# The last tile of a decoder layer: gated rows copied and multiplied in pieces, fewer identity turnings, and a tie factor joined to a multiplication

## The chip, the cores and the metric

The kernel is written in Bass for one NeuronCore of a Trainium2 chip and runs on that one core. What counts is the device time of one execution in microseconds. The kernel before took 554.35 us (median of three runs, 554.33 to 556.05). The engines by their short names: PE is TensorE, DVE VectorE, ACT ScalarE, POOL GpSimd, SP SyncE, which here only issues loads and stores.

## The reference

One layer of a decoder on x of 1024 rows by 128: self-attention with 16 heads, cross-attention of the 1024 rows to 6404 rows of context under a mask, and a feed-forward part whose operands are quantised to four bits in blocks of 16. The change touches only the last.

```python
def fp4_quant_dequant(x):
    xb = x.reshape(shape[:-1] + (shape[-1] // BLOCK, BLOCK))
    scale = jnp.max(jnp.abs(xb), axis=-1, keepdims=True) / 6.0
    scale = jnp.maximum(scale, jnp.float32(1e-12))
    xn = xb / scale
    idx = jnp.searchsorted(_MID, jnp.abs(xn))
    q = _GRID[idx] * jnp.sign(xn) * scale
...
x = x + _L0_xattn_ref(_layernorm(x, axis=-1), ctx_1024, mask_BxSxS2_ik0, L0_xattn_W, L0_xattn_b)
x = x + _L0_ffn_ref(_layernorm(x, axis=-1), ...)
# in _L0_ffn_ref, with fp4_linear(x, w) = quantised x times quantised w:
gate = fp4_linear(x, w_gate)
y = fp4_linear(x, w_up)
h = jax.nn.silu(gate) * y
return fp4_linear(h, w_down)
```

The grid is 0, 0.5, 1, 1.5, 2, 3, 4, 6, and a value in the middle between two points goes to the lower one.

## The kernel before

The five engines each run a program that is written out by hand, in the order in which its instructions stand; semaphores alone tie them together. The rows are cut into 8 tiles of 128. The self-attention takes the first half of the time; the change does not touch it.

**Cross-attention of a tile t.** The context is cut into 13 chunks of 512 columns. For each chunk PE makes the logits in one of two banks (`logits`, three products), DVE adds the mask, takes the maximum and writes them to SBUF (`masked`, L878), ACT takes the exponential, PE turns them (L1240), ACT copies them (L690) and PE multiplies them with the context (`pv_chunk`). The logits run ahead of the rest by seven chunks and a tile. A bank of logits is free for PE when L878 on it is done. POOL makes summands out of the mask's integers in pieces of 1024 columns (L524); SP loads the pieces into a ring of four. At the end of a tile DVE adds the result to x (`finish_tile`, L893).

**Feed-forward of a tile**, `ffn_step(t, c)`, is woven into the chunks c of the next tile's cross-attention on every engine. Step 0: mean and variance on DVE, the root on POOL (L511). Step 1: DVE normalises (L923) and quantises xn. Step 3: PE turns xn (L1280), ACT copies it (L710). Step 4: the gate product and ACT's tanh (L713). Steps 5 and 6: DVE makes the gated rows out of gate and up (L928, L933). Steps 7 and 8: DVE quantises them, 352 columns. Step 9: PE turns them in three pieces (128, 128 and 96 columns, L1293) into bank 7, and ACT copies the three pieces to hT (L718). Step 10: PE multiplies the three pieces with the down weights into bank 7. Step 11: DVE adds the product to x (L942), and SP stores it. PE does these products with the helper at L975, which so carries most matmuls; one 128x128 product in float32 shows as two matmuls.

`quantize` (L898) is a chain of instructions of DVE, each waiting for the one before (`link`): the greatest of each block of 16 (L905), the scale (L906), its reciprocal (L907), times the factor `TIE_DOWN`, a little below one, so that ties go down (L908), the rows times that (L909); then four steps that round to the grid (L911 to L914) and the multiplication with the scale (L915). It runs twice for each tile, on 8 blocks of xn and on 22 blocks of gated rows, and at step 1 it stands in DVE's order ahead of the `masked` of the same chunk.

**The last tile** has no cross-attention beside its feed-forward part. There PE fills two waits with turnings of the identity into a bank nobody reads (`keep_warm`, L978): `TAIL_NORM` of them ahead of all, and `TAIL_HIDDEN` ahead of step 9. Its up product goes to bank 6, right behind the gate.

```python
pv_chunk(NT * NC - 1)
keep_warm(TAIL_NORM, 0)
for c in range(NC):
    if c == 9:
        keep_warm(TAIL_HIDDEN, 0)
    ffn_step(NT - 1, c)
```

Of the kernel before, what the change touches and what calls it, by code (L numbers as in the profile page):

```python
# [7 lines left out]
ALU = mybir.AluOpType  # L8
# [25 lines left out]
def decoder_layer(nc, x, ctx, mask, w_q, w_k, w_v, w_o, w_down_kv, w_up_k, w_up_v,  # L34
# [6 lines left out]
    NT = S // P  # L41
# [30 lines left out]
    EARLY_MASKS = 6  # L72
    WARM_UP = 28
    KEEP_WARM = 4
    TAIL_NORM = 44
    TAIL_HIDDEN = 56
    LEAD = 7

    with ExitStack() as stack:
# [219 lines left out]

        def logits_bank(n):  # L300
            return 4 + n % 2 if n < NC else n % 2

        def up_bank(t):
            return 6 if t == NT - 1 else 7
# [262 lines left out]
        def _(act):  # L567
# [139 lines left out]
            def ffn_step(t, c):  # L707
                if c == 3:
                    act.wait_ge(s_f4, t + 1)
                    act.activation(xqT[:, :], PS[:, 7, 0:P], ACT.Copy).then_inc(s_f5, 1)  # L710
                if c == 4:
                    act.wait_ge(s_f6, 2 * t + 1)
                    act.activation(fa[:, 0, :], PS[:, 7, 0:FF], ACT.Tanh, scale=0.5).then_inc(s_f7, 1)  # L713
                if c == 9:
                    act.wait_ge(s_f9, t + 1)
                    for j in range(NF):
                        w = min(P, FF - j * P)
                        last = act.activation(hT[0:w, j, :], PS[0:w, 7, j * P:(j + 1) * P], ACT.Copy)  # L718
                    last.then_inc(s_f10, 1)

            for e in range(NE):
# [19 lines left out]
        def _(dve):  # L741
            chain = [0]

            def link(ins):
                chain[0] += 1
                ins.then_inc(dch, 1)
                dve.wait_ge(dch, chain[0])
# [150 lines left out]
            def quantize(dst, src, rows, nb, done, parts=(0, 1)):  # L898
                xs = src.rearrange("p (b k) -> p b k", k=BLOCK)
                sc, inv = f_small[0:rows, 0, 0:nb], f_small[0:rows, 1, 0:nb]  # L900
                wide = lambda a: a.unsqueeze(2).broadcast_to([rows, nb, BLOCK])
                v, pw, s2 = (fa[0:rows, i, 0:nb * BLOCK] for i in (1, 2, 3))
                b3 = lambda a: a.rearrange("p (b k) -> p b k", k=BLOCK)
                if 0 in parts:
                    link(dve.tensor_reduce(sc, xs, axis=AX.X, op=ALU.max, apply_absolute_value=True))  # L905
                    link(dve.tensor_scalar(sc, sc, 1.0 / 6.0, 1e-12, ALU.mult, ALU.max))  # L906
                    link(dve.reciprocal(inv, sc))  # L907
                    link(dve.tensor_scalar(inv, inv, TIE_DOWN, None, ALU.mult))  # L908
                    link(dve.tensor_tensor(b3(v), xs, wide(inv), ALU.mult))  # L909
                if 1 in parts:  # L910
                    link(dve.tensor_scalar(pw.bitcast(I32), v.bitcast(I32), 0x7F800000, None, ALU.bitwise_and))  # L911
                    link(dve.tensor_scalar(pw, pw, 1.0, ROUNDER, ALU.max, ALU.mult))
                    link(dve.tensor_tensor(s2, v, pw, ALU.add))  # L913
                    link(dve.tensor_tensor(v, s2, pw, ALU.subtract))  # L914
                    dve.tensor_tensor(b3(dst), b3(v), wide(sc), ALU.mult).then_inc(done, 1)  # L915

            def ffn_step(t, c):
                if c == 0:
                    moments(t, x_sb[:, t, :])
                    dve.tensor_scalar(mv[:, t, 1:2], mv[:, t, 1:2], LN_EPS, None, ALU.add).then_inc(s_f1, 1)  # L920
                if c == 1:
                    dve.wait_ge(s_f2, t + 1)
                    link(dve.tensor_scalar(xn[:, t, :], x_sb[:, t, :], mv[:, t, 0:1], rstd[:, t:t + 1],  # L923
                                           ALU.subtract, ALU.mult))
                    quantize(xn[:, t, :], xn[:, t, :], P, D // BLOCK, s_f3)
                if c == 5:
                    dve.wait_ge(s_f7, t + 1)
                    dve.scalar_tensor_tensor(fb[:, 0, :], fa[:, 0, :], 1.0, PS[:, 7, 0:FF], ALU.add,  # L928
                                             ALU.mult).then_inc(s_fg, 1)
                if c == 6:  # L930
                    dve.wait_ge(s_f6, 2 * t + 2)
                    dve.wait_ge(s_fg, t + 1)
                    dve.scalar_tensor_tensor(fb[:, 1, :], fb[:, 0, :], 0.5, PS[:, up_bank(t), 0:FF], ALU.mult,  # L933
                                             ALU.mult).then_inc(s_fh, 1)
                if c == 7:
                    dve.wait_ge(s_fh, t + 1)
                    quantize(fb[:, 2, :], fb[:, 1, :], P, FF // BLOCK, s_f8, (0,))
                if c == 8:
                    quantize(fb[:, 2, :], fb[:, 1, :], P, FF // BLOCK, s_f8, (1,))
                if c == 11:  # L940
                    dve.wait_ge(s_f11, t + 1)
                    dve.tensor_tensor(x_sb[:, t, :], x_sb[:, t, :], PS[:, 7, 0:D], ALU.add).then_inc(s_f12, 1)  # L942

            for s in range(EARLY_SLOTS):
                if early_rows(s) is not None:
# [27 lines left out]
        def _(pe):  # L973
            def mm(o, a, b, start=True, stop=True, alone=False):
                return pe.matmul(o, a, b, start=start, stop=stop, skip_group_check=alone)  # L975
# [297 lines left out]
            def ffn_step(t, c):  # L1273
                if c == 3:
                    pe.wait_ge(s_f3, t + 1)
                    if t == 0:
                        pe.wait_ge(s_fwc, 2 * NF + 1)
                    else:
                        pe.wait_ge(s_f12, t)
                    pe.transpose(PS[:, 7, 0:P], xn[:, t, :], ident[:, :]).then_inc(s_f4, 1)  # L1280
                if c == 4:
                    pe.wait_ge(s_f5, t + 1)
                    mm(PS[:, 7, 0:FF], xqT[:, :], wguT[:, 0, :]).then_inc(s_f6, 1)
                    if t == NT - 1:
                        mm(PS[:, up_bank(t), 0:FF], xqT[:, :], wguT[:, 1, :]).then_inc(s_f6, 1)
                if c == 6 and t < NT - 1:
                    pe.wait_ge(s_fg, t + 1)
                    mm(PS[:, up_bank(t), 0:FF], xqT[:, :], wguT[:, 1, :]).then_inc(s_f6, 1)
                if c == 9:
                    pe.wait_ge(s_f8, t + 1)  # L1290
                    for j in range(NF):
                        w = min(P, FF - j * P)
                        last = pe.transpose(PS[0:w, 7, j * P:(j + 1) * P], fb[:, 2, j * P:j * P + w], ident[:, :])  # L1293
                    last.then_inc(s_f9, 1)
                if c == 10:
                    pe.wait_ge(s_f10, t + 1)
                    for j in range(NF):
                        w = min(P, FF - j * P)
                        last = mm(PS[:, 7, 0:D], hT[0:w, j, :], wdT[0:w, j, :], start=(j == 0), stop=(j == NF - 1))
                    last.then_inc(s_f11, 1)  # L1300

            for t in range(4, NT):
# [47 lines left out]
```

## Time and profile before

| what | value |
|---|---|
| runs | 554.35, 556.05, 554.33 us |
| the profiled execution | 554.33 us |
| its span, first to last instruction | 552.6 us |
| mean granted clock of PE | 0.963 of full speed |
| PE, DVE, ACT, POOL busy | 499.6 (90%), 362.4 (66%), 336.2 (61%), 171.1 (31%) us |
| chain that ended last, by engine | PE 72%, DVE 20%, issue 3%, DMA 2%, ACT 2% |

The span is 1.7 us shorter than the execution's own time. A granted clock of 1.00 is PE's level of 2.4 GHz, 0.50 that of 1.2 GHz; a mean between the two says that a part of the stretch ran at the lower one. A busy share is a mean over stages with different limits, so it does not tell what a change in one place is worth.

### The profile page before, as it was taken

How to read it: one execution, taken by the hardware profiler on the slowest of the kernel's cores; microseconds unless marked ns; L12 is line 12 of the kernel's file. 1: busy time of each engine (PE TensorE's matmuls, PEld its weight loads, DVE VectorE, ACT ScalarE, POOL GpSimd, SP SyncE). 2: the span in 40 equal slices, each digit the busy share in tenths (PEclk: the TensorE clock that was granted, in tenths of full speed). 3: DMA queues.
4: the chain of work that ended last, by engine and by line, in shares of the span. 5: the costliest groups of instructions: out<-in, count | busy, mean ns of one | idle time of the engine just before them, and what ended most of it. 6: DMA issues, size and time to landing. Idle time of an engine off the chain costs nothing.

```text
span 552.6 us, 9809 instructions
## 1 busy us (share of the span) xinstructions
PE 499.6 (90%) x3494; PEld 327.1 (59%) x3494; DVE 362.4 (66%) x874; ACT 336.2 (61%) x659; POOL 171.1 (31%) x292
## 2 busy tenths in 40 slices
PE   8359999999999999989979979989797997989997
PEld 7206333333333333324549979879797997878886
DVE  6889988888788878704454466646666465654344
ACT  4627778787778777876664826537373562737420
POOL 6810125444444453235442221321222122210000
PEclk9758999999999999999999989989999998999999
DMA  8985400051007000031696423333342333300000
GB/s 243 284 256 121 88 2 2 4 134 41 1 3 166 10 2 2 1 117 39 165 325 187 124 76 116 93 114 92 83 121 79 116 91 115 114 16 6 1 6 7
DMA packets 27957, 49.23 MB, mean 89 GB/s; under 512 B 4140, under 2 KB 15860, under 8 KB 27332
## 3 DMA queue, kind: packets, MB, share of 16 engines
q1 hardware_dynamic: 27156, 47.87, 31.3%
q0 software_dynamic: 224, 0.54, 0.4%
q8 instruction: 28, 0.46, 0.4%
q10 hardware_dynamic: 528, 0.18, 0.2%
q14 instruction: 21, 0.17, 0.1%
HBM read 43.67 MB, written 4.72 MB: 88 GB/s over the span
## 4 chain that ended last, share of the span: by engine, by line
PE 72%; DVE 20%; issue 3%; DMA 2%; ACT 2%; POOL 1%; SPq 0%; DVEq 0%; ACTq 0%; POOLq 0%
PE banks L975 48%; PE banks L1084 11%; PE banks L1240 6%; DVE banks L802 6%; PE banks L1095 2%; DVE logits L878 2%; DVE fa L914 1%; PE banks L980 1%; DMA operands<-query_parts 1%; DVE qc_lo L849 1%; DVE xn L923 1%; DVE fa L913 1%; DVE fa L909 1%; ACT probs L669 1%; DVE f_small L905 1%
## 5 line engine op out<-in xcount | busy, mean ns | idle before, releaser
L669 ACT ACTIVATE probs<-banks 128x512 f32<-128x512 f32 x288 | 160.2, 599 | 49.1 <-PE banks L975 43.5
L802 DVE CUSTOM_DVE_ANT_0 banks<-banks,decay 128x1024 f32<-128x1024 f32 x128 | 155.0, 1244 | 31.4 <-PE banks L975 30.8
L975 PE MATMUL banks<-operands 112*128 112x512 bf16 (+4 forms) x736 | 148.0, 332 | 21.2 <-DMA operands<-query_parts 14.2
L975 PEld LDWEIGHTS banks<-operands 115*128 115x128 bf16 (+1 forms) x736 | 55.2, 98 | 126.9 <-ACT probs L669 55.1
L975 PEld LDWEIGHTS banks<-mem,pT 128*128 128x128 f32 (+1 forms) x816 | 108.5, 196 | 7.9
L975 PE MATMUL banks<-mem,pT 128*128 128x128 f32 (+1 forms) x816 | 112.1, 280 | 0.0
L690 ACT ACTIVATE pT<-banks 128x512 f32<-128x512 f32 (+1 forms) x104 | 60.4, 581 | 53.7 <-PE banks L1240 53.7
L878 DVE CUSTOM_DVE_ANT_0 logits<-banks,mring 128x512 f32<-128x512 f32 (+1 forms) x85 | 56.2, 667 | 43.2 <-PE banks L975 22.0
L532 POOL TENSOR_SCALAR_AFFINE_SELECT probs<-probs 128x128 f32<-128x128 f32 x128 | 37.3, 294 | 108.8 <-ACT probs L669 106.9
L1084 PE MATMUL banks<-probs,v_ext 128*32 128x512 f32 x512 | 68.2, 605 | 0.1
L975 PE MATMUL banks<-memT_hi,qc_hi 128*128 128x512 f32 (+1 forms) x104 | 51.0, 491 | 18.7 <-DVE cmax L878 18.7
L524 POOL TENSOR_SCALAR mring<-mring 128x1024 f32<-128x1024 int32 (+1 forms) x46 | 43.8, 953 | 75.0 <-DMA mring<-in_mask_BxSxS_ik 72.9
L1240 PE MATMUL banks<-ident,logits 128*128 128x128 f32 (+1 forms) x408 | 63.2, 278 | 0.0
L680 ACT ACTIVATE logits<-logits,neg_max 128x1024 f32<-128x1024 f32 (+1 forms) x56 | 58.8, 1050 | 0.0
L1240 PEld LDWEIGHTS banks<-ident,logits 128*128 128x128 f32 (+1 forms) x408 | 49.4, 144 | 4.1 <-issue 2.2
L511 POOL TENSOR_TENSOR rstd<-mv,half_neg 128x1 f32<-128x1 f32 x16 | 8.8, 551 | 129.7 <-DVE mv L920 83.6
L975 PE MATMUL banks<-memT_hi,qc_lo 128*128 128x512 f32 (+1 forms) x104 | 41.3, 397 | 0.0
L975 PE MATMUL banks<-memT_lo,qc_hi 128*128 128x512 f32 (+1 forms) x104 | 41.2, 396 | 0.0
L538 POOL TENSOR_SCALAR_AFFINE_SELECT probs<-probs 128x512 f32<-128x512 f32 x32 | 20.5, 641 | 42.7 <-ACT probs L669 42.7
L975 PEld LDWEIGHTS banks<-memT_hi,qc_hi 128*128 128x128 f32 x104 | 20.5, 198 | 21.5 <-DVE cmax L878 20.9
L710 ACT ACTIVATE xqT<-banks 128x128 f32<-128x128 f32 x8 | 2.2, 278 | 36.8 <-PE banks L1280 36.8
L975 PEld LDWEIGHTS banks<-memT_hi,qc_lo 128*128 128x128 f32 x104 | 20.2, 194 | 4.4
(170 smaller groups left out, 515.4 us busy)
## 6 DMA issues: line engine op xcount, KB each, us to landing
mring<-in_mask_BxSxS_ik SPq DMA_DIRECT2D x39, 512.0 KB, 3.5
operands<-key_parts SPq DMA_DIRECT2D x24, 192.0 KB
operands<-query_parts SPq DMA_DIRECT2D x21, 192.0 KB
key_parts<-operand_parts SPq DMA_DIRECT2D x10, 256.0 KB, 3.3
mem<-in_ctx SPq DMA_DIRECT2D x3, 832.0 KB, 8.9
mask<-in_mask_BxSxS_ik SPq DMA_DIRECT2D x9, 256.0 KB, 2.9
pT<-in_mask_BxSxS_ik SPq DMA_DIRECT2D x9, 256.0 KB, 3.0
query_parts<-operand_parts SPq DMA_DIRECT2D x4, 384.0 KB, 5.3
```

The costliest lines, as they stand in the source:

```text
L524: pool.tensor_scalar(src.bitcast(F32), src, -1.0, -NEG, ALU.add, ALU.mult).then_inc(s_ma, 1)
L532: pool.affine_select(out=diag, in_=diag, compare_op=ALU.is_ge, fill=0.0, base=0, pattern=[[1, P]], channel_multiplier=-1).then_inc(s_sel, 1)
L538: pool.affine_select(out=upper, in_=upper, compare_op=ALU.is_ge, fill=0.0, base=-1, pattern=[[0, HG], [-1, P]], channel_multiplier=1).then ...
L669: act.activation(probs[:, to, :], PS[:, u % 3, :], ACT.Exp).then_inc(s_p, 1)
L680: act.activation(y, y, ACT.Exp, bias=neg_max[:, t:t + 1], accum_out=esum[:, t, e:e + 1]).then_inc(s_e, 1)
L690: last = act.activation(pT[:, n % 3, 0:o], PS[:, 2 + n % 2, 0:o], ACT.Copy)
L802: dve.tensor_tensor_reduce(out=rows, in0=rows, in1=decay[:, off:off + S], scale=1.0, scalar=-3.0e38, op0=ALU.mult, op1=ALU.max, accum_out= ...
L878: dve.tensor_tensor_reduce(out=logits_sb(t)[:, k0:k0 + kw], in0=PS[:, logits_bank(n), 0:kw], in1=mk, scale=1.0, scalar=-3.0e38, op0=ALU.ad ...
L975: return pe.matmul(o, a, b, start=start, stop=stop, skip_group_check=alone)
L1084: last = pe.matmul(PS[h * VW:(h + 1) * VW, 3, :], v_ext[:, kt, g * HG + h, :], probs[:, (gb % 2) * HG + i, :], start=(b % NT == 0), stop=( ...
L1095: last = pe.matmul(PS[h * VW:(h + 1) * VW, 3, d0:d0 + P], v_ext[:, kt, g * HG + h, :], probs[:, 2 * HG + n % 2, h * P:(h + 1) * P], start= ...
L1240: last = pe.transpose(PS[0:kw, 2 + n % 2, j * P:(j + 1) * P], logits_sb(t)[:, k * P:k * P + kw], ident[:, :])
```

## The change

Three edits, and numbers that go with them:

- `quantize` joins the factor to the multiplication: L908 and L909 become one scalar_tensor_tensor, (xs times `TIE_DOWN`) times the reciprocal. This holds for all 16 quantisations of DVE.
- In the last tile ACT signals each of its three copies, PE waits for each piece ahead of the piece's product, and the product goes to bank 6 (`down_bank`), from where DVE adds it.
- `TAIL_NORM` goes from 44 to 40, `TAIL_HIDDEN` from 56 to 46.

```diff
-    TAIL_NORM = 44
-    TAIL_HIDDEN = 56
+    TAIL_NORM = 40
+    TAIL_HIDDEN = 46
...
+        def down_bank(t):
+            return 6 if t == NT - 1 else 7
...
                     for j in range(NF):
                         w = min(P, FF - j * P)
                         last = act.activation(hT[0:w, j, :], PS[0:w, 7, j * P:(j + 1) * P], ACT.Copy)
+                        if t == NT - 1 and j < NF - 1:
+                            last.then_inc(s_f10, 1)
                     last.then_inc(s_f10, 1)
...
-                    link(dve.tensor_scalar(inv, inv, TIE_DOWN, None, ALU.mult))
-                    link(dve.tensor_tensor(b3(v), xs, wide(inv), ALU.mult))
+                    link(dve.scalar_tensor_tensor(b3(v), xs, TIE_DOWN, wide(inv), ALU.mult, ALU.mult))
...
-                    dve.tensor_tensor(x_sb[:, t, :], x_sb[:, t, :], PS[:, 7, 0:D], ALU.add).then_inc(s_f12, 1)
+                    dve.tensor_tensor(x_sb[:, t, :], x_sb[:, t, :], PS[:, down_bank(t), 0:D], ALU.add).then_inc(s_f12, 1)
...
                 if c == 10:
-                    pe.wait_ge(s_f10, t + 1)
                     for j in range(NF):
+                        if t == NT - 1:
+                            pe.wait_ge(s_f10, t + 1 + j)
+                        elif j == 0:
+                            pe.wait_ge(s_f10, t + 1)
                         w = min(P, FF - j * P)
-                        last = mm(PS[:, 7, 0:D], hT[0:w, j, :], wdT[0:w, j, :], start=(j == 0), stop=(j == NF - 1))
+                        last = mm(PS[:, down_bank(t), 0:D], hT[0:w, j, :], wdT[0:w, j, :], start=(j == 0), stop=(j == NF - 1))
```

In the changed kernel the lines of these functions stand 3 to 5 further down. PE's program at its end, before (L980 turns the identity, L1280 xn, L1293 the gated rows `fb`; hqT_ready is `s_f10`):

```order
L980 MATMUL banks<-ident 128x128 x44
L1280 MATMUL banks<-ident,xn 128x128 [waits y_ready,xq_ready]
L975 MATMUL banks<-wguT,xqT 128x352 [waits xqT_ready]
L975 MATMUL banks<-wguT,xqT 128x352
L980 MATMUL banks<-ident 128x128 x56
L1293 MATMUL banks<-ident,fb 128x128 [waits hq_ready]
L1293 MATMUL banks<-ident,fb 128x128
L1293 MATMUL banks<-ident,fb 96x128
L975 MATMUL banks<-wdT,hT 128x128 [waits hqT_ready]
L975 MATMUL banks<-wdT,hT 128x128 x2
```

The same place of the changed kernel:

```order
L984 MATMUL banks<-ident 128x128 x40
L1284 MATMUL banks<-ident,xn 128x128 [waits y_ready,xq_ready]
L979 MATMUL banks<-wguT,xqT 128x352 [waits xqT_ready]
L979 MATMUL banks<-wguT,xqT 128x352
L984 MATMUL banks<-ident 128x128 x46
L1297 MATMUL banks<-ident,fb 128x128 [waits hq_ready]
L1297 MATMUL banks<-ident,fb 128x128
L1297 MATMUL banks<-ident,fb 96x128
L979 MATMUL banks<-wdT,hT 128x128 [waits hqT_ready] x3
```

Nothing changes its place; the two blocks are shorter, and each of the three down products has a wait of its own. On DVE the chain of a quantisation has 9 instructions where it had 10.

## Rows read from the trace of the kernel before

**Rows 1.** The page, chain that ended last, by line.
```profile
PE banks L975 48%; PE banks L1084 11%; PE banks L1240 6%; DVE banks L802 6%; PE banks L1095 2%; DVE logits L878 2%; DVE fa L914 1%; PE banks L980 1%; DMA operands<-query_parts 1%; DVE qc_lo L849 1%; DVE xn L923 1%; DVE fa L913 1%; DVE fa L909 1%; ACT probs L669 1%; DVE f_small L905 1%
```
**Rows 2.** Busy time by stretch, one stretch a tile (stretch, length, engines, clock).
```profile
353.58:387.32 33.74, 30.93 (x213) 28.16 (x213) 20.62 (x63) 17.26 (x37) 7.80 (x9) 0.95 0.35 101
387.32:419.53 32.21, 29.33 (x213) 26.71 (x213) 20.68 (x63) 17.27 (x37) 7.81 (x9) 1.00 0.36 105
...
513.55:535.06 21.51, 19.59 (x165) 18.43 (x165) 9.30 (x30) 8.31 (x18) 0.55 (x1) 1.00 0.01 4
```
**Rows 3.** Waits of PE, 320 to 552.6 us (us in total, times, longest).
```profile
PE banks L975 <- DVE cmax L878: 16.3, 6, 2.9
PE banks L1293 <- DVE fb L915: 2.5, 3, 0.9
PE banks L1280 <- DVE xn L915: 1.2, 2, 1.0
```
**Rows 4.** Timeline, boundary of tile 1 (start us, length us, engine, line, instruction).
```profile
355.72 1.15 DVE L923 TENSOR_SCALAR xn<-x_sb,mv,rstd 128x128 f32<-128x128 f32 x1
355.75 1.54 POOL L524 TENSOR_SCALAR mring<-mring 128x1024 f32<-128x1024 int32 x2
...
357.67 0.17 DVE L908 TENSOR_SCALAR f_small<-f_small 128x8 f32<-128x8 f32 x1
...
358.73 0.29 DVE L913 TENSOR_TENSOR fa<-fa 128x128 f32<-128x128 f32 x1
359.01 1.04 POOL L524 TENSOR_SCALAR mring<-mring 128x1024 f32<-128x1024 int32 x1 [1.73 <-DMA mring<-in_mask_BxSxS_ik]
359.05 1.14 DVE L914 TENSOR_TENSOR fa<-fa 128x128 f32<-128x128 f32 x1
360.23 0.29 DVE L915 TENSOR_TENSOR xn<-fa,f_small 128x128 f32<-128x128 f32 x1
...
361.18 0.50 PE L975 MATMUL banks<-memT_hi,qc_hi 128*128 128x512 f32 x1 [2.81 <-DVE cmax L878]
```
**Rows 5.** Timeline, boundary of tile 2.
```profile
392.67 0.29 DVE L913 TENSOR_TENSOR fa<-fa 128x128 f32<-128x128 f32 x1
392.81 1.06 POOL L524 TENSOR_SCALAR mring<-mring 128x1024 f32<-128x1024 int32 x1 [2.06 <-DMA mring<-in_mask_BxSxS_ik]
393.00 1.01 DVE L914 TENSOR_TENSOR fa<-fa 128x128 f32<-128x128 f32 x1
```
**Rows 6.** Timeline, boundary of tile 5, DVE.
```profile
492.66 0.29 DVE L914 TENSOR_TENSOR fa<-fa 128x128 f32<-128x128 f32 x1
```
**Rows 7.** Timeline, the last tile's feed-forward part.
```profile
540.07 0.33 PE L1280 MATMUL banks<-ident,xn 128*128 128x128 f32 x1 [0.17 <-DVE xn L915]
...
542.05 6.28 PE L980 MATMUL banks<-ident 128*128 128x128 f32 x56
...
544.43 0.18 DVE L908 TENSOR_SCALAR f_small<-f_small 128x22 f32<-128x22 f32 x1
...
547.08 0.52 DVE L915 TENSOR_TENSOR fb<-fa,f_small 128x352 f32<-128x352 f32 x1
548.06 0.35 PEld L1293 LDWEIGHTS banks<-ident,fb 128*128 128x128 f32 x3
...
548.69 0.60 ACT L718 ACTIVATE hT<-banks 128x128 f32<-128x128 f32 x3 [6.57 <-PE banks L1293]
...
549.35 0.94 PE L975 MATMUL banks<-wdT,hT 128*128 128x128 f32 x6 [0.69 <-ACT hT L718]
```
**Rows 8.** Timeline of ACT, a window that holds only the third copy.
```profile
549.03 0.27 ACT L718 ACTIVATE hT<-banks 96x128 f32<-96x128 f32 x1
```
**Rows 9.** Groups of DVE by line and form (busy us, mean ns, idle before).
```profile
L909 DVE TENSOR_TENSOR fa<-fb,f_small 128x352 f32<-128x352 f32 x8 | 4.2, 525 | 0.3
...
L933 DVE SCALAR_TENSOR_TENSOR fb<-fb,banks 128x352 f32<-128x352 f32 x8 | 4.2, 521 | 17.4 <-PE banks L975 17.3
L893 DVE SCALAR_TENSOR_TENSOR x_sb<-banks,rden,x_sb 128x128 f32<-128x128 f32 x8 | 2.8, 351 | 18.2 <-PE banks L975 18.2
```

## Prediction

> **What bounds the kernel now.** I read first the chain that ended last, by line. The matmuls of the helper line L975 carry most of it, but a fifth of the span is VectorE, spread over lines of about 1% each, the quantisation (L909, L913, L914) among them [rows 1]. The change touches only the feed-forward part, which runs one tile behind the cross-attention, so the question is where that part's VectorE work reaches the path.
>
> The second view is the busy time by stretch, one stretch for each tile, from one addition L893 to the next. TensorE is busy for about 31 us of 33.7; the next tile takes 32.2 us. The difference between these two is not work: both have 213 matmuls, and the granted clock is 0.95 in the one and 1.00 in the other [rows 2]. So a stretch at the lower level of the clock (1.2 instead of 2.4 GHz) costs some 1.6 us of a tile. Of the five such tiles (boundaries 0 to 4) four are like the first row, and only the one from 387.32 is at 1.00.
>
> The third view is what TensorE waited for from 320 us on: six times for the masked logits of L878, 16.3 us in all and 2.9 at the longest, three times for the quantised hidden rows (2.5 us), twice for the quantised input rows (1.2 us) [rows 3]. Nothing else there is large.
>
> The fourth is the timeline at such a wait for L878. The logits' banks are freed by L878, which stands in VectorE's order behind the whole quantisation of xn. TensorE starts at 361.18, right behind the first L878 after L915. Look at L923 and L914: 1.15 and 1.14 us, where the like L913 takes 0.29. Each overlaps a mask piece of POOL (L524, at 355.75 and 359.01); L914 ends 0.14 us after that piece's end [rows 4]. At the next tile's boundary the same holds, with L914 at 393.00 and the piece at 392.81 [rows 5]. I read the boundaries of tiles 0 to 4, and they are alike but for one distance: 0.17 to 0.21 us from the piece's start to L914's at tiles 0, 2, 3 and 4, but only 0.04 at tile 1. At tile 5 no mask is left and L914 takes 0.29 [rows 6].
>
> **The factor joined to the multiplication.** Each of 16 quantisations loses one small instruction. L908 lasts 0.17 us on 8 columns and 0.18 on 22 [rows 4, 7], and behind each link the next instruction starts some 0.03 later (L913 ends at 359.02, L914 starts at 359.05 [rows 4]): 0.20 and 0.21 us. What takes L909's place is a scalar_tensor_tensor. Its price here with two operands from SBUF is not in the trace. Nearest rows: on 128x352 L909 takes 525 ns, and L933, of the new kind with one operand from PSUM, 521; on 128x128 L893, which also takes a scalar per row, 351 [rows 9] against 0.29 of the tensor_tensor L913 [rows 4]. I take no difference, as L933 is nearest in form (an immediate factor); the ends are a gain of nothing and a loss of 0.06 each.
>
> Where does this land? In seven quantisations VectorE is what TensorE waits for, with no piece of POOL between: the hidden rows of tile 4, both quantisations of tiles 5, 6 and 7. Three narrow ones and four wide ones: 3 x 0.20 + 4 x 0.21 = **1.44 us**.
>
> At the boundary of tile 1, L914 would start at 358.85, 0.16 before POOL's piece. L913 at 392.67 started 0.14 before the piece and took its plain 0.29 [rows 5], so L914 gets through, and L915 behind it meets the piece and ends, as L914 did before, 0.14 after it: 360.19 instead of 360.52. That gives **0.33 us** (lower end 0).
>
> At the boundaries of tiles 0, 2, 3 and 4, L914 would start within 0.04 us of the piece's start. L923 at 355.72 started 0.03 before a piece and was held all the same [rows 4]. So L914 is still held, its end is set by POOL, and the saved 0.20 us vanishes: **0** (other end 0.33 each). The piece itself does not move: its load is issued behind the first L878 of the boundary, ahead of the quantisation. Here a rule speaks otherwise. The Trainium skill (SBUF — State Buffer, Who interferes with whom) says of this pair of engines that a VectorE instruction with two SBUF inputs and a GpSimd instruction that reads SBUF exclude each other, the first to issue having the port for its whole length. That the later one waits, the trace agrees; that the first start by the record decides, the row at 355.72 denies. By that rule L914 would pass at tile 0, and at the others on a hundredth of a microsecond, and the sum would be up to 1.3 us larger.
>
> The other quantisations of hidden rows (tiles 0 to 3) end with slack before TensorE's turning, which waits only three times [rows 3]; what hides them is TensorE's own logits and products. Were that cover gone they would give 0.21 us each.
>
> **Fewer identity turnings.** The second block (56) runs from 542.05 to 548.33, so about 0.11 us a turning. VectorE has the hidden rows at 547.60 (L915), yet TensorE's first weight load of them is at 548.06 [rows 7]: the block overruns. Behind a plain wait TensorE starts 0.06 after what it waited for (the products at 549.35, behind copies that end at 549.29), so the overrun costs 548.06 - 547.66 = **0.40 us**. With 46 the block ends 1.1 us sooner, and 0.2 more as all begins sooner: about 547.0, before the rows, now due at 547.60 - 0.41 = 547.19. The first block (44 to 40) did not hold: L1280 waited 0.17 us for xn [rows 7]; the cut of 0.45 keeps that so when xn comes 0.20 sooner. Zero by itself.
>
> **Piece by piece.** Now TensorE waits for the three copies as a whole: 548.69 to 549.29, and starts at 549.35; its six half-products take 0.94 [rows 7]. One copy lasts 0.27 [rows 8], so they start 0.165 apart, and the first is there at +0.27. With the same 0.06 the products start at +0.33 instead of +0.66. The second and third pieces (+0.44, +0.60, and 0.06) are there before their pairs are due (0.11 a half: +0.55, +0.77). Gain **0.33 us**; lower end 0.2 if each of the two added waits costs a hand-over. Writing to bank 6 costs nothing: its last reader is L933, long before; in bank 7 the product would overwrite pieces yet to be copied. Two added semaphore increments on ScalarE hold up nobody. Behind the waits stands only the product itself, and for it only L942 and the last store.
>
> **The sum.** 1.44 + 0.33 + 0.40 + 0.33 = 2.50 us, of which 0.41 + 0.40 + 0.33 = 1.14 falls in the last tile. The profiled execution took 554.33 us (span 552.6), which is also the lowest of the three and 0.02 below their median: **551.8 us**, 0.45% less. About 0.3% (1.7 us) is what a measurement of this kernel can tell from no change. The third run, 556.05, stands 1.7 higher, close to the 1.6 us of one low stretch of the clock.
>
> **The rivals.**
> 1. *The clock decides otherwise.* Waits of 2.8 to 2.9 us ended at the low level at four of the five boundaries of tiles 0 to 4, and not at tile 2, though the waits are of one length [rows 2, 3]. Length alone does not decide, so moving the work by some tenths may win or lose one stretch: 551.8 - 1.7 = 550.1, or 551.8 + 1.7 = 553.5. For it: the spread of the three runs. Against: four waits keep their length to a few hundredths, and the first moves not at all. Chance 0.12 for one fewer, 0.14 for one more.
> 2. *L914 slips ahead of the mask piece* at tiles 0, 2, 3 and 4, so that L915 is the one held: 4 x 0.33 = 1.3 more, 550.5, and with shorter waits perhaps a low stretch less, 548.8. For it: the margins are 0.01 to 0.04 us. Against: the row at 355.72. Chance 0.13. The rule of the Trainium skill named above is this case.
> 3. *The change does little outside the last tile*: the new instruction costs 0.2 more than L909, eating what L908 gave. Then only 0.40 + 0.33 are left, with 0.33 of tile 1 gone: 553.6. Rows 9 speak against it. Chance 0.05.
> 4. *Slower: the clock falls in the last tile*, because the blocks of turnings no longer reach up to the work behind them. Idle of about 0.4 us before L1280 and 0.2 before the hidden rows' turning takes their place. If the level then stays low to the end, what lies between L1280 (540.07) and the second block (542.05) takes up to 2.0 us more, and the 46 turnings take 10.1 us instead of 5.1 [rows 7]: they end near 541.85 + 2.0 + 10.1 = 553.95, 6.8 us after the hidden rows are due, and the turnings of the hidden rows (0.63) and the products (0.94) double too. In all 8.4 us more, 560.2. It decides from the first fall at all; one short fall, as at the boundaries, would cost at most 1.7. Against it: in the tile before, waits of 1.0 and 0.9 us left the clock at 1.00 [rows 2, 3]. Chance 0.03.
>
> **How the numbers follow.** The forecast has the remaining 0.53. It, the fewer-stretches case and rival 2 are below 552.7: 0.78 faster. One stretch more and rival 3 lie between: 0.19 same. Rival 4: 0.03 slower. The range, 549.9 to 553.6, holds the forecast with its bounds (the sum between 1.6 and 3.8), one stretch either way and rival 3; it leaves out rival 4 and the far half of rival 2.
>
> **What would show it** (by the line numbers of before). Right: L908 has no row, and the step from L907 to L911 is shorter by 0.20; at tile 1 L914 takes 0.29 and L915 is long; at tiles 0, 2, 3, 4 L914 is still about 1.0 and TensorE's wait still 2.9; tile 5's wait is 0.2 shorter; in the last tile the first load of the hidden rows follows their last multiplication by 0.06, and the products start 0.33 after the first copy. Wrong: L915 in L914's place at the four other boundaries (rival 2), another number of tiles near 33.8 us (rival 1), a longer multiplication (3), a granted clock below 1.00 behind 535 us (4).

## The result and the profile after

The changed kernel took 549.88 us in the median of 6 runs (548.67 to 552.64), the kernel before 554.95 (6 runs, 553.57 to 556.05): a ratio of 0.9911, with a 95% interval of 0.9882 to 0.9940. Taken again with six more runs (e12 below) it was 549.47 and 0.9901 (0.9881 to 0.9921). So it is faster, by 5.1 and 5.0 us, twice what was forecast; 549.88 lies 0.02 below the forecast's range. The profiled execution took 550.32 us, with a span of 548.6.

First view: busy time by stretch, one stretch from one tile's addition (now L898) to the next, and at the end to the last addition (L946). Columns as in [rows 2]: stretch and length, busy us (and instructions) of PE, PE's weight loads, DVE, ACT, POOL, then the granted clock, the DMA share and GB/s.

```profile
320.86:352.77 31.91, 29.23 (x213) 26.68 (x213) 20.42 (x61) 17.25 (x37) 7.90 (x9) 1.00 0.35 106
352.77:386.24 33.47, 30.87 (x213) 28.20 (x213) 20.35 (x62) 17.24 (x37) 7.77 (x9) 0.95 0.35 101
386.24:418.16 31.92, 29.24 (x213) 26.66 (x213) 20.42 (x61) 17.24 (x37) 7.89 (x9) 1.00 0.37 106
418.16:451.70 33.54, 30.87 (x213) 28.20 (x214) 20.42 (x62) 17.25 (x37) 7.92 (x9) 0.95 0.35 101
451.70:485.51 33.81, 30.65 (x210) 27.78 (x210) 19.77 (x56) 16.73 (x35) 7.22 (x8) 0.95 0.35 100
485.51:511.17 25.66, 23.22 (x184) 21.49 (x184) 13.49 (x41) 15.62 (x33) 2.00 (x3) 1.00 0.02 4
511.17:532.27 21.10, 19.61 (x165) 18.44 (x165) 8.95 (x29) 8.30 (x18) 0.55 (x1) 1.00 0.01 4
532.27:546.33 14.06, 12.68 (x100) 11.10 (x99) 8.42 (x25) 1.34 (x5) 0.55 (x1) 1.00 0.00 1
```

The same eight stretches of before are 33.83, 33.74, 32.21, 33.81, 34.14, 26.07, 21.51 and 15.26 us, 230.57 in all; now 225.47. The gain is 5.1 us behind the first addition; ahead of it, where the code is the same, this execution happened to be 1.1 us later. Two things are to be seen. The first stretch is shorter by 1.92 us, and its clock is now 1.00: one stretch at the low level is gone (three tiles at 0.95, not four). And where the clock is the same, a cross-attention tile is still 0.27 to 0.33 us shorter, tiles 5 and 6 (the 25.66 and 21.10) 0.41 each, and the last one 1.20.

Second view: the waits of PE from 320.8 us on, which answer to [rows 3].

```profile
PE banks L979 <- DVE cmax L883: 15.1, 6, 2.7
PE banks L1297 <- DVE fb L919: 2.0, 4, 0.7
PE banks L1284 <- DVE xn L919: 1.2, 2, 0.8
```

The six waits for the masked logits fell by 0.2 us each (0.15 at tile 4), where the prediction had four of them unchanged. The third view says why: the timeline at the boundary of tile 2, which answers to [rows 5] (L918 is the old L914, L919 the old L915, L883 the old L878).

```profile
391.38 0.29 DVE L917 TENSOR_TENSOR fa<-fa 128x128 f32<-128x128 f32 x1
391.71 0.29 DVE L918 TENSOR_TENSOR fa<-fa 128x128 f32<-128x128 f32 x1
391.75 1.15 POOL L527 TENSOR_SCALAR mring<-mring 128x1024 f32<-128x1024 int32 x1 [2.10 <-DMA mring<-in_mask_BxSxS_ik]
392.03 1.01 DVE L919 TENSOR_TENSOR xn<-fa,f_small 128x128 f32<-128x128 f32 x1
...
393.70 0.50 PE L979 MATMUL banks<-memT_hi,qc_hi 128*128 128x512 f32 x1 [2.68 <-DVE cmax L883]
```

L918 starts 0.04 us ahead of the mask piece and takes its plain 0.29; now the piece waits for it (1.15 us instead of 1.06) and L919 is the one that is held. At tiles 0 and 3 the margins are 0.03 and 0.01, and it goes the same way. At tiles 1 and 4 the piece came later from the addition than in the kernel before (5.54 us instead of 5.43, and 5.67 instead of 5.47), so L918 was clear of it, the piece took its plain 1.04, and L919 was held until 0.14 behind the piece's end. At tile 1:

```profile
358.03 0.29 DVE L918 TENSOR_TENSOR fa<-fa 128x128 f32<-128x128 f32 x1
358.31 1.04 POOL L527 TENSOR_SCALAR mring<-mring 128x1024 f32<-128x1024 int32 x1 [1.84 <-DMA mring<-in_mask_BxSxS_ik]
358.35 1.14 DVE L919 TENSOR_TENSOR xn<-fa,f_small 128x128 f32<-128x128 f32 x1
```

From the addition to PE's first logits behind the wait: 7.46 us at tiles 0, 2 and 3, 7.39 at tile 1, 7.52 at tile 4, 6.25 at tile 5; before 7.68, 7.67, 7.67, 7.60, 7.66 and 6.46.

Fourth view: the timeline of the last tile, which answers to [rows 7].

```profile
537.07 0.33 PE L1284 MATMUL banks<-ident,xn 128*128 128x128 f32 x1 [0.41 <-DVE xn L919]
...
539.05 5.18 PE L984 MATMUL banks<-ident 128*128 128x128 f32 x46
...
543.86 0.52 DVE L919 TENSOR_TENSOR fb<-fa,f_small 128x352 f32<-128x352 f32 x1
544.44 0.30 PEld L1297 LDWEIGHTS banks<-ident,fb 128*128 128x128 f32 x3 [0.44 <-DVE fb L919]
...
545.03 0.60 ACT L721 ACTIVATE hT<-banks 128x128 f32<-128x128 f32 x3 [5.90 <-PE banks L1297]
545.36 0.94 PE L979 MATMUL banks<-wdT,hT 128*128 128x128 f32 x6 [0.37 <-ACT hT L721]
```

The block of 46 ends at 544.23, ahead of the hidden rows at 544.38, and their turning follows 0.06 behind them. The products start 0.33 behind the first copy, not 0.66. The joined instruction costs what the multiplication cost: 0.29 and 0.52 us (at 535.22 and 541.43). All of this is as forecast.

### The profile page after: what moved, and what is told of

Same layout as the page of the kernel before. It is cut to its first block, busy times and chain, and to the rows that moved or that the text cites. A ratio compares the mean times of both kernels' runs of the same rounds, so it can differ in the third digit from the quotient of the medians.

```text
span 548.6 us, 9765 instructions
## 1 busy us (share of the span) xinstructions
PE 497.0 (91%) x3480; PEld 324.7 (59%) x3480; DVE 360.2 (66%) x858; ACT 335.9 (61%) x659; POOL 170.9 (31%) x292
## 4 chain that ended last, share of the span: by engine, by line
PE 71%; DVE 17%; DMA 6%; issue 2%; POOL 2%; ACT 2%; SPq 0%; DVEq 0%; POOLq 0%; ACTq 0%
PE banks L979 49%; PE banks L1088 11%; PE banks L1244 6%; DVE banks L807 6%; DMA mring<-in_mask_BxSxS_ik 3%; DVE logits L883 2%; PE banks L1099 2%; DMA operands<-query_parts 1%; POOL mring L527 1%; DMA x_sb<-in_x 1%; ACT probs L672 1%; PE banks L1151 1%; PE banks L1297 1%; DVE fa L913 1%; DMA query_parts<-operand_parts 1%
## 5 line engine op out<-in xcount | busy, mean ns | idle before, releaser
L883 DVE CUSTOM_DVE_ANT_0 logits<-banks,mring 128x512 f32<-128x512 f32 (+1 forms) x85 | 56.2, 666 | 42.9 <-PE banks L979 26.7
```

The lines of the kernel that those rows point to most:

```text
L883: dve.tensor_tensor_reduce(out=logits_sb(t)[:, k0:k0 + kw], in0=PS[:, logits_bank(n), 0:kw], in1=mk, scale=1.0, scalar=-3.0e38, op0=ALU.ad ...
```

## The experiments

Two theories were set against each other. A: the joined factor shortens every boundary through the order of starts at POOL's mask piece, and with shorter waits there are fewer stretches at the low clock. B: the boundaries are as they were (or don't matter), and the excess over the forecast is luck with the clock.

| kernel | median us (runs) | runs of before taken beside it, median us | first L893 to last addition, us |
|---|---|---|---|
| before, profiled | | | 230.57 |
| the change | 549.88 (6) | 554.95 | 225.47 |
| e1, join alone | 550.04 (6) | 555.67 | 225.73 |
| e2, last tile's edits alone | 555.39 (12) | 555.67 | 230.01 |
| e3, joined for hidden rows alone | 553.74 (12) | 555.67 | 230.30 |
| e4, joined for xn alone | 551.79 (12) | 555.67 | 227.39 |
| e5, numbers of turnings alone | 553.82 (1) | 554.91 | 230.00 |
| e7, xn's quantisation split | 536.64 (4) | 554.91 | 211.78 |
| e8, mask piece a memset | 541.45 (1) | 554.91 | 217.32 |
| e9, change with turnings in the waits | 544.26 (4) | 554.91 | 220.51 |
| e10, before with turnings in the waits | 546.93 (5) | 554.45 | 223.58 |
| e11, shorter chain of xn | 536.45 (1) | 554.45 | 213.34 |
| e12, the change again | 549.47 (6) | 554.45 | 225.43 |

The last column is read in each kernel's profile. A kernel with one run is read by its profile and not by its time.

**e1: the join alone.** Undone: the two numbers, the signals and waits by piece, bank 6.

```diff
-    TAIL_NORM = 40
-    TAIL_HIDDEN = 46
+    TAIL_NORM = 44
+    TAIL_HIDDEN = 56
...
-            return 6 if t == NT - 1 else 7
+            return 7
...
-                        if t == NT - 1:
-                            pe.wait_ge(s_f10, t + 1 + j)
-                        elif j == 0:
-                            pe.wait_ge(s_f10, t + 1)
```

> The changed kernel with the last tile's edits undone (44 and 56 turnings, one wait for the three copies, bank 7); only the joined factor is left. Theory A (the saved 0.2 us lets the rounding subtraction of xn start ahead of POOL's mask piece, so every boundary of tiles 0 to 4 gains 0.2): from the addition of tile t to TensorE's first logits behind the wait 7.46 us at tiles 0 to 4 where before had 7.60 to 7.68, 6.25 at tile 5; the last tile (addition to last addition) 15.26 to 15.06, since the hidden rows come 0.41 sooner but the block of 56 turnings still overruns them. Sum without the clock: 5 x 0.21 at the boundaries, 0.21 at tile 5, 3 x 0.21 for hidden rows, 0.2 each for tiles 6 and 7: about 2.3 us less than before. Theory B (the gain beyond the last tile is only the number of stretches at the low clock): boundaries as before, and a median within 1.2 us of before. Under both, a tile with a low stretch is 1.6 us longer than one without.

The boundaries are 7.48, 6.55, 7.47, 7.47, 7.47 and 6.26, the last tile 15.06: A within 0.02, but for tile 1. There the mask piece came late enough that even the multiplication got ahead of it. The timeline at that place (L916 and L917 are the old L914 and L915):

```profile
359.20 0.29 DVE L916 TENSOR_TENSOR fa<-fa 128x128 f32<-128x128 f32 x1
359.53 0.29 DVE L917 TENSOR_TENSOR xn<-fa,f_small 128x128 f32<-128x128 f32 x1
359.59 1.14 POOL L527 TENSOR_SCALAR mring<-mring 128x1024 f32<-128x1024 int32 x1 [1.95 <-DMA mring<-in_mask_BxSxS_ik]
```

Here 0.06 us of margin was worth another 0.9 us. The ratio is 0.991 (0.9884 to 0.9937), the change's own, so most of the gain sits in the join; the 0.8 us of the last tile's other edits (e2) is less than these intervals can tell. The median is 5.6 us below before, where A's sum was 2.3. What is missing can be read from the mean granted clock of each run: one low stretch moves it by 0.003 (0.963 with four behind the boundaries, 0.966 with three, by the profiles), and these six runs had on average 1.0 stretches fewer than four, the 29 of before beside them 0.6 more. That is 1.6 stretches of 1.6 us, 2.6 us; 0.7 of the 5.6 stays open. Such a count does not say where in the kernel the stretches lay. The profile of e7 has one at 255 us, in the self-attention, which no other kept profile has.

**e2: the last tile's edits alone.**

```diff
-                    link(dve.scalar_tensor_tensor(b3(v), xs, TIE_DOWN, wide(inv), ALU.mult, ALU.mult))
+                    link(dve.tensor_scalar(inv, inv, TIE_DOWN, None, ALU.mult))
+                    link(dve.tensor_tensor(b3(v), xs, wide(inv), ALU.mult))
```

> The changed kernel with the factor as an instruction of its own again: only the last tile's edits are left. Boundaries of tiles 0 to 4 as before, 7.60 to 7.68 us, tile 5 6.46; the last tile 15.26 - 0.40 - 0.33 = 14.5 us. Theory A: 0.75 us less than before in the median, times scattered by the 1.6 us of a low stretch as before's are. Theory B (the clock's stretches make the size): the same 0.75 here, but then the join alone cannot reach 4 us either, unless it changes the number of low stretches.

The last tile took 14.48 us, as expected, and the boundaries were 7.64 to 7.72. The ratio is 0.9998 (0.9981 to 1.0016): 0.78 us is too little for these runs to show, the more so since they had 0.3 low stretches more than before's; the profile shows it.

**e3 and e4: the join for one of the two quantisations.** Both have the last tile as before, and in `quantize`, for e3:

```diff
+                    if nb == FF // BLOCK:
+                        link(dve.scalar_tensor_tensor(b3(v), xs, TIE_DOWN, wide(inv), ALU.mult, ALU.mult))
+                    else:
+                        link(dve.tensor_scalar(inv, inv, TIE_DOWN, None, ALU.mult))
+                        link(dve.tensor_tensor(b3(v), xs, wide(inv), ALU.mult))
```

e4 has `nb < FF // BLOCK` in the condition.

> Before with the factor joined in the quantisation of the hidden rows (22 blocks) only. Both theories: boundaries as before (7.60 to 7.68), since xn's chain is unchanged; 0.21 less in tiles 5 and 6 and in the tile that follows tile 4's boundary, nothing in the last tile, where the block of 56 turnings holds the hidden rows: 0.6 us less in all. Number of low stretches as before, 4 or 5.

> Before with the factor joined in the quantisation of xn (8 blocks) only. Theory A: 0.21 less at each of the five boundaries of tiles 0 to 4, 0.2 at tile 5, 6 and in the last tile: 1.6 us less, the subtraction behind the rounding addition takes 0.29 and the multiplication behind it about 1.0; POOL's piece at the boundary takes 1.15 to 1.19 us instead of 1.05 because it now waits for the subtraction. Theory B: 0.33 at tile 1 only, 0 at tiles 0, 2, 3, 4, and 0.6 in tiles 5 to 7.

e4 agrees with A at tiles 0 and 3 (7.46) and has 7.26 at tile 1. At tiles 2 and 4 (7.54 and 7.61) the mask piece came first, by 0.12 and 0.03 us, and the subtraction was held (1.07 and 1.15 us), as the prediction had it. At tile 4 (L920 is the old L914):

```profile
457.96 1.05 POOL L527 TENSOR_SCALAR mring<-mring 128x1024 f32<-128x1024 int32 x1 [2.02 <-DMA mring<-in_mask_BxSxS_ik]
457.99 1.15 DVE L920 TENSOR_TENSOR fa<-fa 128x128 f32<-128x128 f32 x1
```

So which of the two cases comes depends on when the mask's load lands. Over the five profiles with the joined chain and a wait at the boundary (the change, e1, e4, e9, e12) the subtraction was first at 17 of the 20 boundaries of tiles 0, 2, 3 and 4. The profile of e4 has three low stretches at the boundaries. Its ratio is 0.9952 (0.9930 to 0.9975), its median 3.9 us below before: A's 1.6, and 1.0 low stretches fewer (1.7 us), with 0.6 left open. e3 kept four low stretches in its profile and boundaries of 7.67 to 7.83, but for tile 1 with 7.50, where its mask piece came 0.2 us later than before's and L914 got ahead. Its ratio is 0.9969 (0.9951 to 0.9986): 1.9 us for an expected 0.6, and by the clock 0.8 low stretches fewer (1.3 us). xn's half carries most. But e3's runs had fewer low stretches although the waits at the boundaries in its profile are not shorter than in before's (2.72 to 3.04 us against 2.81 to 2.90), so the length of those waits is hardly all that sets the number.

**e5: the numbers of turnings alone.**

```diff
-    TAIL_NORM = 44
-    TAIL_HIDDEN = 56
+    TAIL_NORM = 40
+    TAIL_HIDDEN = 46
```

> Before with only the numbers of turnings changed, 40 and 46. The last tile takes 15.26 - 0.40 - 0.04 = 14.8 us: the block ends ahead of the hidden rows and their turning follows VectorE by 0.06. Rival: the first cut costs something, the last tile 15.0 or more. With the tail's two edits together at 14.48, what is left for the pieces is 0.33.

The last tile took 14.80: 0.46 less. With e2's 14.48 the pieces are left with 0.32.

**e8: POOL writes, but doesn't read.** The mask of tiles 1 on is left out of the result (the first six chunks of tile 1 keep theirs).

```diff
-                pool.tensor_scalar(src.bitcast(F32), src, -1.0, -NEG, ALU.add, ALU.mult).then_inc(s_ma, 1)
+                pool.memset(src.bitcast(F32), 0.0).then_inc(s_ma, 1)
```

> Before with POOL's mask pieces of tiles 1 on (L524) made a plain memset to 0 instead of arithmetic on the loaded integers: the mask of those tiles is left out, and POOL writes but doesn't read the ring. All waits stay. Theory A (VectorE's instructions with two operands in SBUF are held by POOL's reading of SBUF): L914 at the boundaries takes 0.29 instead of 1.0, the boundary 7.67 - 0.75 = about 6.9 us or, with L849 and L923 free too, 6.0 to 6.3. Theory B (the long L914 has nothing to do with what POOL reads): 1.0 again while a memset of the same length runs. A memset that is much shorter than 1.05 us would weaken the test; its length is read in the trace.

The boundaries are 6.32, 6.61 and four times 6.32 to 6.33. The timeline at tile 0:

```profile
321.98 1.33 POOL L524 MEMSET mring<- 128x1024 f32 x2
322.06 0.29 DVE L849 TENSOR_TENSOR qc_lo<-qc,qc_hi 128x128 fp32r<-128x128 f32 x1
322.27 0.73 DVE L923 TENSOR_SCALAR xn<-x_sb,mv,rstd 128x128 f32<-128x128 f32 x1
```

L849, a tensor_tensor with two operands from SBUF, began 0.08 us after the memset and took 0.29; beside the arithmetic of POOL it takes 1.13 in the kernel before. L923, a tensor_scalar, is still held (0.73, where it takes 0.35 with no POOL instruction beside it). So whether POOL reads is what matters for the one, and not for the other. The Trainium skill (SBUF — State Buffer, Who interferes with whom) says that two SBUF inputs contend with a GpSimd instruction that reads SBUF, and a tensor_scalar in its two-port mode with any. The 0.29 and 0.73 agree; in which mode L923 runs no trace shows. L914 itself ended ahead of the memset here, so on L914 the test says nothing: it began 0.64 us earlier at tile 0 (5.04 instead of 5.68 us from the addition) and was clear of the piece. Its neighbour L915 was behind the memset once, at tile 1 (356.63 against 356.55), and took its plain 0.29.

**e9 and e10: the clock kept up.** Twenty turnings of the identity in the wait ahead of the logits of chunk 3, in the changed kernel (e9) and in before (e10):

```diff
+                    if t in range(1, 6) and c == 3:
+                        keep_warm_at(20)
                     if n < NT * NC:
                         logits(n)
```

> The changed kernel with 20 identity turnings on TensorE in the wait of each boundary of tiles 1 to 5's chunk 3 (2.2 us of the 2.6 to 2.7 of wait; tile 5's 1.7 is overrun by 0.5), into a part of bank 6 nobody reads. Nothing else is moved. Theory A (each boundary's wait is what brings the clock down, and a low stretch costs 1.6 us): no low stretch from 320 to 540 us in the profile, tiles of 31.9 us each, and a median 3 x 1.6 - 0.5 = about 4 us below the changed kernel, 546 us, with runs scattered less. Theory B (low stretches come from elsewhere, or cost nothing of themselves): as many of them, 550 us.

> Before with the 20 identity turnings in the boundaries' waits (the same insertion that was made to the changed kernel), so that the clock stays up in both and their difference is the change without the clock. Theory A (of some 5 us, about 3.4 are the change itself: 5 x 0.21 at boundaries, 0.2 at tile 5, 5 quantisations of 0.2 in tiles 4 to 6, 1.2 in the last tile; the rest is one to two low stretches fewer): no low stretch from 320 us on, tiles of 32.2 us at boundaries 0 to 3, and a median 3.4 above the changed kernel with turnings, 547.7 us. Theory B (the change itself brings the whole 5 us): 549.3 us.

The granted clock is 1.00 in all tiles of both. The first and the fourth stretch of e9, then the same of e10:

```profile
319.58:351.61 32.03, 31.44 (x233) 28.85 (x233) 20.52 (x61) 17.24 (x37) 7.78 (x9) 1.00 0.37 106
...
415.36:447.42 32.06, 31.43 (x233) 28.86 (x233) 20.56 (x62) 17.25 (x37) 7.79 (x9) 1.00 0.36 106
```

```profile
319.32:351.69 32.37, 31.50 (x233) 28.88 (x233) 20.86 (x64) 17.26 (x37) 7.80 (x9) 1.00 0.36 105
...
415.89:448.09 32.20, 31.49 (x233) 28.88 (x233) 20.71 (x63) 17.27 (x37) 7.84 (x9) 1.00 0.37 105
```

More work on PE made before 7.5 us faster and the change 5.4 (medians 554.45 to 546.93, and 549.7 of all twelve runs to 544.26). The turnings stand at the boundaries of tiles 0 to 4 alone, so tile 5's overrun, which the expectation of e9 takes into account, doesn't exist. The difference of the two is the change without the clock: 223.58 - 220.51 = 3.07 us between the additions, 2.7 between the medians (taken on different chips). Theory A had 3.4. The remaining 2 us of the 5.0 go with the clock: they are gone when neither kernel has a low stretch.

**e7: the wait itself taken apart.**

```diff
-                    quantize(xn[:, t, :], xn[:, t, :], P, D // BLOCK, s_f3)
+                    quantize(xn[:, t, :], xn[:, t, :], P, D // BLOCK, s_f3, (0,))
+                if c == 2:
+                    quantize(xn[:, t, :], xn[:, t, :], P, D // BLOCK, s_f3, (1,))
```

> The changed kernel with the quantisation of xn split as that of the hidden rows already is: scaling ahead of the masked logits of chunk 1, the four rounding steps ahead of those of chunk 2. Theory A (TensorE's wait at a boundary is VectorE's unbroken chain ahead of L878's counterpart, and the low clock stretches follow from that wait): the waits of 2.7 us fall below 1.5 at all of tiles 0 to 4 (the chain ahead of the first masked logits is 1.5 us shorter and misses POOL's piece), in place of them a second, shorter wait may appear a chunk later; no low stretch behind a boundary any more; 1.5 x 5 + 1.6 x 3 = about 12 us less than the changed kernel, 538 us. Theory B (the wait moves whole to the next chunk, since two banks of logits cover only one chunk): same time as the changed kernel within 2 us, 550.

536.64 us, ratio 0.9665 (0.9637 to 0.9693): faster than both kernels. The waits of PE from 321 us on:

```profile
PE banks L981 <- DVE cmax L883: 3.0, 6, 0.6
PE banks L1286 <- DVE xn L919: 2.7, 7, 0.8
```

The six waits of 15.1 us are down to 3.0, no tile has a low stretch, and the new wait for xn (seven times, 2.7 us) is the small price.

**e11: a chain shorter by 0.44 us.** The scale's floor and its reciprocal are left out for xn, whose rows are then multiplied by the block's greatest value.

```diff
-                    link(dve.tensor_scalar(sc, sc, 1.0 / 6.0, 1e-12, ALU.mult, ALU.max))
-                    link(dve.reciprocal(inv, sc))
+                    if nb == FF // BLOCK:
+                        link(dve.tensor_scalar(sc, sc, 1.0 / 6.0, 1e-12, ALU.mult, ALU.max))
+                        link(dve.reciprocal(inv, sc))
+                    else:
+                        inv = sc
```

> The changed kernel with two further small instructions left out of the quantisation of xn only (the scale's factor and floor, and its reciprocal: the greatest of each block is used in their place), so its chain is 0.44 us shorter. Theory A (what counts is which instructions start ahead of POOL's mask piece): the multiplication behind the rounding now starts 0.1 or more ahead of the piece and is not held: boundaries of tiles 0 to 4 from 7.46 to about 6.3 us, 1.16 less for 0.44 saved, and with waits of 1.5 us no low stretch; tile 5, where there is no piece, only 0.44 less, 5.81. Theory B (each saved tenth is a tenth): 7.02 at tiles 0 to 4.

Boundaries 6.30, 6.10, 6.30, 6.31, 6.30, and 5.81 at tile 5; no low stretch at any. At tile 1 (L921 and L922 are the old L914 and L915):

```profile
354.71 0.29 DVE L921 TENSOR_TENSOR fa<-fa 128x128 f32<-128x128 f32 x1
355.04 0.29 DVE L922 TENSOR_TENSOR xn<-fa,f_small 128x128 f32<-128x128 f32 x1
...
355.51 1.05 POOL L527 TENSOR_SCALAR mring<-mring 128x1024 f32<-128x1024 int32 x1 [1.92 <-DMA mring<-in_mask_BxSxS_ik]
...
356.00 0.50 PE L982 MATMUL banks<-memT_hi,qc_hi 128*128 128x512 f32 x1 [1.31 <-DVE cmax L883]
```

0.44 us saved gave 1.16 where there is a mask piece (tiles 0, 2 and 3) and 0.44 where there is none. This settles that what counts is how many instructions start ahead of the piece.

**e12: the change again.**

> The changed kernel once more, for a closer ratio and a second profile. Theory A (which runs have one low stretch fewer is chance, with a mean lower than before's): most runs at a mean granted clock of 0.966, against 0.963 of before, median 549.5 to 550.5, ratio 0.991; boundaries 7.4 to 7.5 again, or about 6.5 where the mask piece comes late. Theory B (the first six runs were lucky): median near 551.8.

Median 549.47. Boundaries 7.46, 7.32, 7.47, 7.46, 7.45, 6.25, and three low stretches once more. Over both sets of the changed kernel 8 of 12 executions have a mean granted clock of 0.965 or 0.966, 2 of 0.968 or 0.969, and 2 of 0.963 and 0.960. Of 47 executions of before that ran beside the experiments, 33 stand at 0.962 or 0.963, 7 at 0.959 or 0.960, 7 at 0.956, and none above 0.963. Counted as in e1, before had on average 0.45 stretches more than four and the change 0.92 fewer: 1.4 stretches, 2.2 us, which is close to the 2 us that e9 and e10 leave for the clock.

## Why the prediction was right and wrong

- **Seven quantisations on the path, 1.44 us: right.** Tile 5's boundary lost 0.21, and tiles 5 and 6 lost 0.41 each in all, two quantisations apiece. The joined instruction cost no more than the one it replaced, so rival 3 falls.
- **Fewer turnings, 0.40: right** (0.46 in e5; the turning of rows that find PE idle is some 0.04 quicker). **Piece by piece, 0.33: right** (0.32). The last tile lost 1.20 for 1.14 forecast. The clock stayed at 1.00 there; rival 4 falls.
- **Tile 1, 0.33: too much.** L914 got ahead as forecast, and L915 ended 0.14 behind the piece, as forecast. But the piece itself began 0.11 us later from the addition than in the kernel before (5.54 instead of 5.43), because its load landed later: 0.21. The step took the piece's start as fixed ("The piece itself does not move"), and over the profiles it moves by up to 0.3 us at this place.
- **Tiles 0, 2, 3 and 4, "L914 is still held ... and the saved 0.20 us vanishes": wrong.** It gained 0.22, 0.21, 0.21 and 0.14. Rival 2, to which I gave 0.13, is what happened, at 0.2 and not 0.33 each: at tiles 0, 2 and 3 the piece now waits for L914 and ends 0.1 us later, and at tile 4 it began 0.2 later. With margins of 0.01 to 0.04 us there was chance in it too: e4 at tiles 2 and 4, and e9 at tile 3, show L914 held as forecast. What failed is the reading of the one row on which I leaned: L923 at 355.72, which looked 0.03 us ahead of the piece and was held. The row of the instruction in front of it, which I had in view and didn't weigh, says otherwise. From the timeline of before:

```profile
355.51 0.29 DVE L849 TENSOR_TENSOR qc_lo<-qc,qc_hi 128x128 fp32r<-128x128 f32 x1
355.72 1.15 DVE L923 TENSOR_SCALAR xn<-x_sb,mv,rstd 128x128 f32<-128x128 f32 x1
```

L849 runs to 355.80, and nothing links L923 to it, so L923's record begins while L849 is still at work. I read this as a start that came in truth behind 355.80, and so behind the piece's 355.75. L914 waits for L913 by a semaphore, so its recorded start is its own. The rule of the Trainium skill (SBUF — State Buffer, Who interferes with whom), that the first to issue has the port for its whole length, held down to 0.01 us at tile 3 (423.62 against 423.63), and I had weighed it against a row that didn't speak of it. The kept traces bear the reading out, though no run was made for it. In e7 a tensor_scalar that does wait for the one in front (L916, the old L912) stands at the piece's start. At tile 3 it began 0.02 us ahead and took its plain 0.23; at tile 0 it began 0.01 behind and was held:

```profile
418.35 0.23 DVE L916 TENSOR_SCALAR fa<-fa 128x128 f32<-128x128 f32 x1
418.37 1.12 POOL L527 TENSOR_SCALAR mring<-mring 128x1024 f32<-128x1024 int32 x1 [2.09 <-DMA mring<-in_mask_BxSxS_ik]
```

```profile
327.10 1.05 POOL L527 TENSOR_SCALAR mring<-mring 128x1024 f32<-128x1024 int32 x1 [2.07 <-DMA mring<-in_mask_BxSxS_ik]
327.11 1.12 DVE L916 TENSOR_SCALAR fa<-fa 128x128 f32<-128x128 f32 x1
```

So it is not the kind of instruction that made L923 an exception. From 300 us on, the thirteen profiles have 103 places where one of the linked steps L911 to L915 (by the lines of before) and a mask piece that reads SBUF overlap: in the 51 where the step's recorded start is first it takes its plain time, and in the 52 where the piece's is first the step is held.

- **The clock: taken as a coin with two even sides (0.12 and 0.14), and it was loaded.** e9 and e10 show what the clock brought: with no low stretch in either kernel the change is worth 3.07 us, without the turnings 5.0. Why the low stretches come less often is not shown. Over the eight profiles with these waits left open (before, the change, e1 to e5, e12), a wait of 2.8 us or more at tiles 0 to 4 was followed by a low stretch at 15 of 19 places, a wait of 2.5 to 2.75 us at 13 of 20; behind a wait of 2.0 us or less (tile 5 everywhere, tile 1 of e1, and e7, e8, e11) there was none. The first two shares are too near each other to say that 0.2 us less of wait is the reason, and e3 speaks against it. A shorter wait is also an earlier one, and no run moves the one without the other. The prediction's "Length alone does not decide" stands; what it had wrong is the chance, which it gave evenly to one stretch fewer and one more. By the count of e12 this is some 2.2 of the 5.0 us.

So the sum without the clock should have been 1.44 + 0.21 + 0.78 + 0.46 + 0.32 = 3.2; e9 and e10 measured 3.07 between the additions. The direction was right for the reasons given; about half of the size was missing, 0.7 us of it in the boundaries and some 2 us in the clock. Open is why, of waits of one length, some bring the clock down and some do not. Open too are 0.06 to 0.08 us by which tiles 1 to 3 got shorter beyond their boundaries, some 0.2 in all.

## What to carry to other kernels

When a chain of short instructions on VectorE runs into a GpSimd instruction, ask which of them starts first: the price comes in steps (0.2 us saved gave 0.21, 0.44 gave 1.16), and the margin stands in the timeline. Read starts only from instructions that wait for the one in front; where one does not, take the end of the one in front. A margin below the 0.3 us by which a load's landing can move is a chance and not a certainty. And where TensorE waits 2 to 3 us again and again, price the clock with the wait: cheap turnings in the waits took 7.5 us off before, and taking the wait apart, by putting half of the chain behind the next masked logits, took 13 us more off the changed kernel.

## What had not been expected of the hardware

- A wait of 2.5 to 3.0 us on TensorE can cost 1.6 us more behind it, in a stretch at 1.2 GHz; of the change's 5.0 us some 2 came this way. Such waits were followed by a low stretch at 28 of 39 places, and none of 2.0 us or less was.
- The landing of one mask load moved by 0.3 us from profile to profile (the piece at tile 1 began 5.37 to 5.66 us after the addition), and through the order of starts that made a boundary 6.55 (e1) instead of 7.39 us (the change).
